# An attention and mixture-of-experts layer: who may hold which pair of PSUM banks

## The chip, the core and the metric

The kernel runs on one core of a Trainium2 chip. Its engines are TensorE (PE: matmuls, with its weight loads shown apart as PEld), VectorE (DVE), ScalarE (ACT), GpSimd (POOL) and the DMA queues of SyncE (SP). They run at the same time and wait for each other by semaphores. The metric is the time of one execution on the device in microseconds (us), less is better.

## The reference, cut to what matters

The layer takes x of 4 x 2048 tokens with 256 features. It is normalised and modulated, goes through causal attention with 16 heads of 16 features, and then through a mixture of 8 experts of which each token takes two. The part that matters here is the attention:

```python
scores = einsum('bhid,bhjd->bhij', q, k)
rel    = einsum('bhid,pd->bhip', q, rel_key)          # 512 relative positions
bias   = take_along_axis(rel, clip(j - i + p - 1, 0, p - 1))
logits = where(j <= i, (scores + bias) * scale, -inf)
out    = softmax(logits) @ v
```

## The kernel before, in words

The program has four phases: modulation, projection, attention, experts. Only the attention phase (`phase_attention`) is touched. It treats the queries in 64 blocks of 128 tokens (16 blocks in each of 4 sequences); block i of a sequence meets the key blocks j = 0 to i. A block of keys within the 512 relative positions is "near" (`near(i, j)`, five of them at most); one further off is "far". A far one has one bias for all its keys, so it needs far fewer matmuls.

Two kinds of work write to PSUM in units of one pair of banks (2 x 512 values on each of 128 partitions):

- **Scores.** For each pair of blocks (number k) two halves, t = 0 and t = 1. PE computes a half (`near_scores` L1161 and L1167, 48 matmuls; `far_scores` L1205, 8 matmuls), ACT reads it with one exponential into `att_pt` (L1126 near, L1129 far). There are 1088 such halves. The 16 matmuls of `weigh` (L1282) then multiply the weights of both halves with the values, into another bank (`att_po`).
- **Maxima.** The softmax's maxima are worked out two blocks ahead, from the same products in another layout: PE computes a half (`near_maxima` L1179 and L1185, 24 matmuls; `far_maxima` L1195, 4 matmuls), and DVE takes the running maximum of it and of `att_acc` (L1039; the first two of a block by two instructions of L1034). There are 1088 of these too, 560 near and 528 far.

Six of the eight banks form `pairs[0..2]` (NPAIR = 3). One more bank, `att_po`, gathers the output, and the last, `att_pk`, serves the single steps: turning the maxima (L1228, read by DVE at L1047), the row of maxima, and the output's normalisation, product and routing (`bank` with the kinds turn, rows, norm, back, out, turn_h, logit, count).

The order of the work is fixed in advance. A planner (`plan`, with `place_time` and `step_time`) spreads the maxima and the single steps over the places of the main loop: score half 0, score half 1, `weigh` of the pair before. `order(...)` walks it once for each engine, and all engines keep it. Before that, one walk calls `take(unit)` for each score half and each half of the maxima. It writes down which pair of banks the unit uses (`pair_of`) and which unit held that pair before (`held_by`). On PE, `pair_free` waits for the reader of the former holder: for ACT's exponential if it was a score half, for DVE's maximum if it was one of the maxima.

Of the kernel before, what the change touches and what calls it, by code (L numbers as in the profile page):

```python
# [36 lines left out]
NB = S // P  # L37
# [612 lines left out]
def phase_attention(nc, io, keep, memory, first):  # L650
# [4 lines left out]
    NPAIR, JT, LEAD = 3, 4, 6  # L655
# [113 lines left out]
    units, pair_of, held_by = [], {}, {}  # L769

    def take(unit):

        pair_of[unit] = len(units) % NPAIR
        held_by[unit] = units[-NPAIR] if len(units) >= NPAIR else None
        units.append(unit)
    order(score=lambda n, j, k, t: take(("scores", t, k)),
          bank=lambda number, behind, kind, *_: take(("maxima", number)) if kind in ("near", "far") else None)

    with memory as a:
# [982 lines left out]
```

How the kernel before makes its waits and increments, by code:

```python
def expand_across(pool, keep, att, n):  # L167
    pool.wait_ge(att.lower, n + 1)
    for part in ACROSS:
        last = expand_groups(pool, keep, att, n, part)
    last.then_inc(att.spread, 1)
    pool.wait_ge(att.spread, n + 1)
# [50 lines left out]
            @block.sync  # L224
# [6 lines left out]
                    sp.dma_start(prj.x[:, it], xv[it]).then_inc(prj.x_first[it], 16)  # L231
                for w, name in ((prj.wq, "wq"), (prj.wk, "wk"), (prj.wv, "wv")):
                    sp.dma_start(w[:, :, :], io[name].rearrange("(e p) n -> p e n", p=P)).then_inc(prj.weights, 16)
                for w, name in ((prj.bq, "bq"), (prj.bk, "bk"), (prj.r0, "r0")):
                    sp.dma_start(w[:, :], io[name]).then_inc(prj.biases, 16)
                sp.dma_start(prj.bv[:, :], io["bv"].partition_broadcast(P)).then_inc(prj.biases, 16)
                sp.wait_ge(pool_step, 1)
                sp.dma_start(io["s_odd"].rearrange("(o p) a -> o (p a)", o=1), odd.rearrange("o e u d v a -> o (e u d v a)")).then_inc(odd_out, 16)
                sp.wait_ge(odd_out, 16)
                sp.dma_start(keep["mask_q"][:, :], io["s_odd"]).then_inc(odd_in, 16)
                sp.wait_ge(odd_in, 16)
                sp.wait_ge(rel_ready, 1)
                sp.dma_start(io["s_rel"][0], relh[:, :]).then_inc(table_out, 16)
                sp.dma_start(io["s_rel"][1], rell[:, :]).then_inc(table_out, 16)
                sp.wait_ge(table_out, 32)
                for i in range(G):
                    seen = slice(G - 1 - i, G - 1 - i + TABW)
```

## Time and profile before

| | |
|---|---|
| median of 3 runs | 3443.24 us (3442.55 to 3448.19) |
| the profiled execution | 3444.56 us, of which the span of its instructions is 3442.5 us |
| busy over the span | PE 2930.0 (85%), PEld 2395.7 (70%), DVE 2277.3 (66%), ACT 1459.2 (42%), POOL 1635.0 (47%) |
| mean granted clock of TensorE | 0.936 of full speed |
| attention phase on PE | from 260.7 us to 2901.1 us |

In the profile each row names a line of the kernel, the engine and the operation, what is written and what is read. PE's time is in two rows: the weight loads (PEld) overlap the matmuls (PE). What stands in brackets behind a row is how long the engine was idle before it and which instruction ended that idle time; "issue" means that nothing in the profile explains it. A unit's matmuls overlap those of the next unit, so the distance between the starts of two units, not the sum of their durations, is what PE spends on one.

### The profile page before, as it was taken

Reading aid. Unit: us, or ns where it says so; the run is one execution under the profiler, and the core shown is the slowest. Engines: PE = TensorE matmul, PEld = TensorE weight load, DVE = VectorE, ACT = ScalarE, POOL = GpSimd, SP = SyncE. Lnnn points to the kernel's source line nnn. Section 1 sums busy time; section 2 is a strip of 40 time slices with the busy share of each in tenths; the row PEclk is TensorE's granted clock in tenths of the full one; section 3 lists DMA queues with packets and bytes.
Section 4 is the critical chain, followed back from the end, with each engine's and each line's share of the span. In section 5 each row is a group of like instructions: output and inputs, shape, how many; then the busy total and the mean of one; then the engine's idle time right before and its main releaser. Section 6 shows DMA issues by size and latency. Waiting matters only on the chain. (4 is left out here: it accounts for less than half of the span.)

```text
span 3442.5 us, 158264 instructions
## 1 busy us (share of the span) xinstructions
PE 2930.0 (85%) x70369; PEld 2395.7 (70%) x70369; DVE 2277.3 (66%) x3796; ACT 1459.2 (42%) x1765; POOL 1635.0 (47%) x1710
## 2 busy tenths in 40 slices
PE   6776899989979998998899989979999995689880
PEld 5445787777768877787787767867877774578760
DVE  6875677776357777744677777357777741666774
ACT  3551334445413344553234444613344453445551
POOL 6665644434475543345655343476444223123647
PEclk8886999999979999998999999989999997899995
DMA  4762222101321110113111110321111001634655
GB/s 117 193 169 64 60 56 54 37 22 42 88 64 45 49 46 24 36 36 107 56 39 51 33 36 24 88 71 54 39 39 36 20 13 37 217 121 153 201 167 145
DMA packets 267455, 253.62 MB, mean 74 GB/s; under 512 B 108073, under 2 KB 227726, under 8 KB 266654
## 3 DMA queue, kind: packets, MB, share of 16 engines
q1 hardware_dynamic: 245246, 201.01, 20.4%
q0 software_dynamic: 20448, 41.45, 4.1%
q8 instruction: 562, 9.21, 1.1%
q14 instruction: 111, 0.91, 0.1%
q10 hardware_dynamic: 1088, 1.05, 0.1%
HBM read 158.83 MB, written 84.46 MB: 71 GB/s over the span
## 5 line engine op out<-in xcount | busy, mean ns | idle before, releaser
L1039 DVE TENSOR_TENSOR att_acc<-att_pair,att_acc 128x1024 f16<-128x1024 f32 x960 | 1164.4, 1221 | 321.9 <-PE att_pair L1185 166.6
L1126 ACT ACTIVATE att_pt<-att_pair 128x1024 f32<-128x1024 f32 x560 | 573.1, 1023 | 1345.6 <-PE att_pair L1167 1345.6
L1282 PE MATMUL att_po<-att_pt,att_vn 128*17 128x128 f32 x17408 | 593.2, 277 | 6.3 <-ACT att_pt L1129 5.1
L1129 ACT ACTIVATE att_pt<-att_pair 128x1024 f32<-128x1024 f32 x528 | 512.3, 1024 | 187.2 <-PE att_pair L1205 183.9
L1282 PEld LDWEIGHTS att_po<-att_pt,att_vn 128*17 128x17 f32 x17408 | 435.4, 98 | 79.7 <-issue 45.4
L182 POOL TENSOR_TENSOR att_qx<-att_qe,mask_i 64x1024 f16<-64x1024 f16 x128 | 239.5, 1884 | 519.2 <-PE att_po L1282 509.7
L1161 PE MATMUL att_pair<-att_qs,att_kn 113*128 113x64 f16 x8960 | 370.8, 196 | 69.6 <-issue 37.9
L1161 PEld LDWEIGHTS att_pair<-att_qs,att_kn 113*128 113x128 f16 x8960 | 314.5, 100 | 143.6 <-issue 90.5
L1167 PE MATMUL att_pair<-att_qx,table_x 68*128 68x64 f16 x8960 | 366.3, 195 | 0.0
L1167 PE MATMUL att_pair<-att_qz,table_z 128*128 128x64 f16 x8960 | 364.4, 195 | 0.3 <-issue 0.2
L1167 PEld LDWEIGHTS att_pair<-att_qx,table_x 68*128 68x128 f16 x8960 | 312.9, 100 | 0.0
L1167 PEld LDWEIGHTS att_pair<-att_qz,table_z 128*128 128x128 f16 x8960 | 310.8, 99 | 0.6 <-issue 0.5
L1034 DVE SCALAR_TENSOR_TENSOR att_acc<-att_pair,bound 128x512 f16<-128x512 f32 x256 | 161.9, 682 | 149.6 <-PE att_pair L1185 149.6
L1179 PE MATMUL att_pair<-att_qq,att_kq 64*128 64x128 f16 x4480 | 229.7, 224 | 24.2 <-DVE att_acc L1039 10.1
L939 POOL TENSOR_TENSOR att_r<-att_ve,att_halfway 128x1 f32<-128x1 f32 x64 | 36.6, 573 | 441.3 <-DVE att_ve L1069 440.9
L182 POOL TENSOR_TENSOR att_qz<-att_qe,mask_i 128x1024 f16<-128x1024 f16 x128 | 239.1, 1884 | 0.0
L1195 PE MATMUL att_pair<-att_qq,att_kq 64*128 64x256 f16 x2112 | 205.6, 276 | 35.4 <-DVE att_acc L1039 34.9
L1185 PE MATMUL att_pair<-att_qy,table_z 64*128 64x64 f16 x4480 | 228.6, 193 | 1.0 <-issue 1.0
L1185 PE MATMUL att_pair<-att_qx,table_x 64*128 64x64 f16 x4480 | 228.5, 193 | 0.2 <-issue 0.2
L1047 DVE TENSOR_REDUCE att_mx<-att_pk 128x4 f32<-128x512 f32 x256 | 175.6, 686 | 76.8 <-PE att_pk L1228 76.2
L1442 POOL TENSOR_TENSOR moe_h_s<-moe_h_f,moe_h_s 128x512 f16<-128x512 f32 x78 | 90.6, 1161 | 254.0 <-ACT moe_h_s L1618 250.6
L1205 PE MATMUL att_pair<-att_qs,att_kn 49*128 49x128 f16 x4224 | 179.7, 217 | 31.1 <-DVE att_acc L1039 16.4
(219 smaller groups left out, 4571.5 us busy)
## 6 DMA issues: line engine op xcount, KB each, us to landing
att_qe<-s_q SPq DMA_DIRECT2D x256, 128.0 KB
moe_xs<-s_h SPq DMA_DIRECT2D x78, 256.0 KB, 3.0
s_y<-moe_y SPq DMA_DIRECT2D x78, 256.0 KB
s_v<-att_vn SPq DMA_DIRECT2D x32, 272.0 KB, 4.3
att_vn<-s_v SPq DMA_DIRECT2D x64, 136.0 KB, 3.0
s_q<-att_kq SPq DMA_DIRECT2D x64, 128.0 KB, 2.2
s_k<-att_kq SPq DMA_DIRECT2D x64, 128.0 KB, 2.4
att_qf<-s_q SPq DMA_DIRECT2D x256, 32.0 KB
```

What stands on the lines that cost most here:

```text
L182: return pool.tensor_tensor(dst[0:rows, s, :, heads, :], att.qe[0:rows, n % 2, heads].rearrange("p h (g i) -> p g h i", i=G), keep["mask_i ...
L1039: dve.tensor_tensor(held, got, held, ALU.max).then_inc(max_done, 1)
L1047: dve.reduce_max(mx[:, n % 2, :].rearrange("p (a c) -> p c a", c=QUADS)[:, r], full[:, :].rearrange("p (h k) -> p h k", k=P), AX.X).then_i ...
L1126: act.activation(pt[:, k % 2, :, t * 64:t * 64 + 64].rearrange("p h (x c) -> p x h c", x=2), full[:, :, :].rearrange("p x (h c) -> p x h c ...
L1129: act.activation(pt[:, k % 2].rearrange("p (e h) c -> p e h c", e=2)[:, :, 4 * t:4 * t + 4], full[:, :, :].rearrange("p e (h c) -> p e h c ...
L1161: pe.matmul(halves[:, x, :, h], kn[0:rows, j, h, :], qs[0:rows, s, :, h, (2 * t + x) * XQ:(2 * t + x + 1) * XQ], start=(h == 0), stop=Fals ...
L1167: last[x] = pe.matmul(groups[:, x, :, g], table[:, y:y + P], moving[:, s, (2 * t + x) * (XQ // G) + g], start=False, stop=(g == XQ // G - ...
L1179: pe.matmul(banks[:, e, c * P:(c + 1) * P], keys[rows, c, :], qq[rows, n % 2, c, :, t * XQ:(t + 1) * XQ], start=(c == 0), stop=False, skip ...
L1185: last[e] = pe.matmul(groups[:, e, g], table[:, y:y + P], moving[:, t * (XQ // G) + g], start=False, stop=(g == XQ // G - 1), skip_group_c ...
L1195: last[e] = pe.matmul(banks[:, e, 2 * c * P:(2 * c + 2) * P], keys[rows, 2 * t + c, :], qq[rows, n % 2, 2 * t + c], start=True, stop=True, ...
L1205: last[e] = pe.matmul(banks[:, e, h * P:(h + 1) * P], kn[rows, j, head, :], qs[rows, s, e, head, :], start=True, stop=True, skip_group_che ...
L1282: last = pe.matmul(po[32 * (h % 4):32 * (h % 4) + VN, h // 4, :], vn[:, j, h, :], pt[:, k % 2, h, :], start=(j == 0 and h < 4), stop=(j == ...
```

## The change

`take` no longer hands out the three pairs in rotation. Half 0 of all scores uses pair 0, half 1 uses pair 1, and all maxima use pair 2. A unit's former holder is the last unit that used the same pair (looked for among the last 128 units). The order of instructions on each engine stays as it was, as do their number, their operands' sizes and all DMAs; what differs is the bank that 2176 units write and read, and the one wait in `pair_free`.

```diff
     def take(unit):
 
-        pair_of[unit] = len(units) % NPAIR
-        held_by[unit] = units[-NPAIR] if len(units) >= NPAIR else None
+        pair_of[unit] = unit[1] if unit[0] == "scores" else NPAIR - 1
+        earlier = [u for u in units[-8 * NB:] if pair_of[u] == pair_of[unit]]
+        held_by[unit] = earlier[-1] if earlier else None
         units.append(unit)
```

## Rows read from the trace of the kernel before

**Rows 1.** Busy time, clock (before the DMA share) by stretch, of all engines.
```profile
260.00:2902.00 2642.00, 2381.64 (x66241) 1967.88 (x66241) 1747.93 (x2705) 1088.10 (x1105) 1243.24 (x1333) 0.96 0.17 47
728.00:782.00 54.00, 49.12 (x1395) 38.88 (x1389) 42.12 (x48) 26.07 (x26) 19.83 (x21) 1.00 0.10 29
950.00:1050.00 100.00, 80.03 (x1965) 69.73 (x1963) 57.43 (x115) 18.54 (x19) 66.88 (x76) 0.82 0.18 53
```

**Rows 2.** Waits of the weight loads, 250 to 2905 us: total us, times, longest.
```profile
PEld att_pair L1195 <- DVE att_acc L1039: 52.0, 81, 1.5
...
PEld att_pair L1161 <- ACT att_pt L1126: 17.4, 32, 0.9
...
PEld att_pk L1228 <- DVE att_mx L1047: 12.9, 15, 1.7
...
PEld att_pair L1179 <- ACT att_pt L1126: 0.2, 1, 0.2
```

**Rows 3.** Timeline of PE from 742 us: start, duration, what.
```profile
742.06 0.39 PE L1195 MATMUL att_pair<-att_qq,att_kq 64*128 64x256 f16 x4 [0.57 <-DVE att_acc L1039]
742.38 1.07 PE L1282 MATMUL att_po<-att_pt,att_vn 128*17 128x128 f32 x32
743.38 0.40 PE L1205 MATMUL att_pair<-att_qs,att_kn 49*128 49x128 f16 x8
743.62 0.39 PE L1179 MATMUL att_pair<-att_qq,att_kq 64*128 64x128 f16 x8
...
744.08 0.39 PE L1205 MATMUL att_pair<-att_qs,att_kn 49*128 49x128 f16 x8
744.39 1.07 PE L1282 MATMUL att_po<-att_pt,att_vn 128*17 128x128 f32 x32
745.39 0.40 PE L1179 MATMUL att_pair<-att_qq,att_kq 64*128 64x128 f16 x8
```

**Rows 4.** Timeline of DVE in the same stretch.
```profile
742.52 1.23 DVE L1039 TENSOR_TENSOR att_acc<-att_pair,att_acc 128x1024 f16<-128x1024 f32 x1
744.31 1.22 DVE L1039 TENSOR_TENSOR att_acc<-att_pair,att_acc 128x1024 f16<-128x1024 f32 x1 [0.56 <-PE att_pair L1185]
```

**Rows 5.** Timeline of PE around 759 us.
```profile
758.18 0.40 PE L1179 MATMUL att_pair<-att_qq,att_kq 64*128 64x128 f16 x8
...
759.08 0.40 PE L1179 MATMUL att_pair<-att_qq,att_kq 64*128 64x128 f16 x8
...
759.64 0.64 PE L1161 MATMUL att_pair<-att_qs,att_kn 113*128 113x64 f16 x16
...
761.15 0.39 PE L1195 MATMUL att_pair<-att_qq,att_kq 64*128 64x256 f16 x4
```

**Rows 6.** Timeline of PE from 729 us.
```profile
729.62 0.40 PE L1179 MATMUL att_pair<-att_qq,att_kq 64*128 64x128 f16 x8
...
730.53 0.40 PE L1179 MATMUL att_pair<-att_qq,att_kq 64*128 64x128 f16 x8
...
731.70 0.40 PE L1205 MATMUL att_pair<-att_qs,att_kn 49*128 49x128 f16 x8 [0.54 <-DVE att_acc L1034]
...
733.35 0.39 PE L1195 MATMUL att_pair<-att_qq,att_kq 64*128 64x256 f16 x4
733.58 0.39 PE L1205 MATMUL att_pair<-att_qs,att_kn 49*128 49x128 f16 x8
733.81 0.38 PE L1195 MATMUL att_pair<-att_qq,att_kq 64*128 64x256 f16 x4
735.34 0.40 PE L1205 MATMUL att_pair<-att_qs,att_kn 49*128 49x128 f16 x8 [1.15 <-DVE att_acc L1039]
...
736.67 0.40 PE L1179 MATMUL att_pair<-att_qq,att_kq 64*128 64x128 f16 x8
```

**Rows 7.** Timeline of DVE in the same stretch.
```profile
730.36 2.47 DVE L1034 SCALAR_TENSOR_TENSOR att_acc<-att_pair,bound 128x512 f16<-128x512 f32 x4
733.46 0.69 DVE L1047 TENSOR_REDUCE att_mx<-att_pk 128x4 f32<-128x512 f32 x1 [0.62 <-PE att_pk L1228]
734.07 2.35 DVE L1039 TENSOR_TENSOR att_acc<-att_pair,att_acc 128x1024 f16<-128x1024 f32 x2
```

**Rows 8.** Timeline of ACT, 742 to 749 us.
```profile
743.85 1.94 ACT L1129 ACTIVATE att_pt<-att_pair 128x1024 f32<-128x1024 f32 x2 [0.91 <-PE att_pair L1205]
```

## The prediction

> **What bounds the kernel now.** I read the stretches by engine first, then PE's waits, then the timeline. Attention takes 2640 of the 3442.5 us of the span, and PE is busy for 2381.6 of 2642 us there, DVE for 1747.9, ACT for 1088.1 [rows 1]. PE is the bound, but DVE is near behind: in the stretch from 728 to 782 us it is busy for 42.1 of 54 us. The waits say what little holds PE up: eleven rows, from 52.0 down to 0.2 us, are weight loads of `att_pair` that waited for ACT or DVE to release a pair of banks, 172.5 us together [rows 2]. Those are the waits that the change deals out anew. The order on PE is fixed, so a late release delays everything behind it, score halves and `weigh` included; nothing overtakes.
>
> **How long one pair is held by a maximum.** A far one: PE starts at 742.06, DVE at 742.52, and it reads for 1.23 us [rows 3, 4]. The next user of a pair starts about 0.05 us after its release (DVE's first of two ends at about 735.28, and PE's idle time at 735.34 [rows 6, 7]), so the cycle is 0.46 + 1.23 + 0.05 = 1.74 us. A near one: 743.62 to 744.31 is 0.69, with 1.22 and 0.05 that makes 1.96 us. With three pairs in rotation the next maximum rarely cares about this, as it takes another pair. With one pair for all maxima, each maximum must start a whole cycle after the one before it. What PE has to do between two maxima is the only cover.
>
> **What PE has between two maxima.** I counted in the written order what stands between each two consecutive maxima, and took the distance of starts from the rows: near maximum to far score 0.46, far score to `weigh` 0.31, `weigh` to the next 1.00, far maximum to `weigh` 0.32 [rows 3]; far maximum to far score 0.23, score to maximum 0.23 [rows 6]; near maximum, one single step, maximum 0.90; near maximum to near score 0.56, near score to maximum 1.51 [rows 5]. A single step after a far maximum I take as 0.65 (0.25 less, as for `weigh`: 0.56 against 0.32). A second far score adds 0.2. What is short is the cycle less this distance:
>
> - nothing between, 30 after a near and 16 after a far maximum: 1.5 us short each, 69 us
> - one single step on `att_pk`, 69 and 28: 1.06 and 1.09 short, 104 us
> - one `weigh`, 60 and 60 (distance 1.56 and 1.32): 0.40 and 0.42 short, 49 us
> - one far score, 20 and 8: 1.27 short, 36 us
> - two far scores, 20 and 12: 1.08 short, 35 us
> - a single step and one or two far scores, 16 and 24: 0.75 short on the mean, 30 us
> - a single step and `weigh`, 32 and 44: 0.08 short, 6 us
>
> That is 329 us from 439 of the 1087 distances. The largest class, 244 maxima with exactly one near score before them, has a distance of 0.56 + 1.51 = 2.07 against 1.96, and some 1.84 against 1.74 after a far one: it is covered, by 0.1 us only. Everything longer is covered.
>
> **What DVE's own queue adds.** DVE also reads the single steps, 0.69 us for a turn [rows 7], in the same order. Where one lies ahead of a maximum, that one is read late, and with a single pair PE can't run ahead to make up for it. I bound this by zero from below. From above, take the trace as it stands: over all 1088 maxima, the time by which the maximum before was still being read (or had not been released for 0.05 us) when the next one started adds up to 414 us, DVE's backlog included; so 85 us at most. Setting the trace's own durations again step by step, with the new releases, I get 383 us in all, that is 54 for this term, and take it. (The same done with the old releases gives 2639.6 us for the phase where the trace has 2639.3, so little is lost in it.)
>
> **What the scores get.** They never wait for DVE any more. Half t now waits for the exponential of the same half of the previous pair. Where far pairs follow with no maximum between them, ACT needs 1.94 us for two exponentials [rows 8] and PE 0.2 + 0.31 + 1.00 = 1.5 us plus whatever step stands there, so ACT can hold a half up by some 0.4 us. The layout gives that 68 times, 27 us; the bounds are 0 and 68 x 0.44 = 30.
>
> **What goes.** All 172.5 us of the old waits are replaced. The single steps wait for DVE too (18 rows for `att_pk`, the first 12.9 us [rows 2], 97 us together); since DVE is less behind when PE stands still more often, some of that goes. I put it at 28 us, from the same layout, between 0 and 97.
>
> **A stretch to check it by.** Maxima start at 729.62 and 730.53. DVE reads each of these first two by two instructions, 2.47 us for four, from 730.36 [rows 6, 7]; so the first is released at 731.60, and the second can't start before 731.65, 1.12 us later than now. The wait of 0.54 us ahead of 731.70 disappears in return. At 733.35 and 733.81 two far maxima stand 0.46 apart; the second must then come 1.74 or more after the first, and the 1.15 us ahead of 735.34 disappear. The maximum at 736.67 comes about 0.9 us later than now. So a stretch of 7 us loses 0.9: new waits are about twice as large as the ones they replace, because the unit that waits stands ahead of score work that had no need to wait.
>
> **The sum.** 329 + 54 + 27 - 172 - 28 = +210 us. The profiled execution took 3444.56 us (2 us around its span), 1.3 us above the median of 3443.24; 3443 + 210 = 3653, with TensorE's clock as it is in the phase, 0.96 on the mean [rows 1]. Rounded: 3655 us.
>
> **A rule that speaks against the change.** The rows show the price of one pair: 1.74 to 1.96 us per maximum, of which PE works on it for less than 0.7. The Trainium skill says under "Perfetto Trace Analysis", section "Optimizing Tensor Performance", that independent groups of matmuls should rotate through different PSUM banks so that reading one out overlaps the next group's matmuls. By that rule the maxima alone lose their rotation, and the scores keep one of two; it gives the direction, and no size.
>
> **Rivals.**
> *The clock falls with PE's business.* From 950 to 1050 us PE is busy for 80.0 of 100 us and the clock is 0.82, while from 728 to 782 it is busy for 49.1 of 54 (0.91) at 1.00 [rows 1]. After the change the phase has 2382/2850 = 0.84 busy. If its mean clock falls from 0.96 to 0.91, PE's work, some 2380 us, takes 130 us more, of which the waits hide a part, say 40: 3745 us. Against it: dense stretches such as 728 to 782 would still be at about 0.82 busy and the new waits are each under 2 us, spread evenly. The Trainium skill ("TensorE: Matmul & The Clock Gate", section "A second HAM failure mode: psum-queue depth-cycling") tells of a kernel that cycled through PSUM banks and lost throughput because short idle times made the clock swing; that would be this rival.
> *The waits overlap more than I think.* If the queue's term is 0 and all 97 us of the single steps' waits go, the sum is 329 + 0 - 172 - 97 = +60, 3503 us; with half of each, 3580. For it speaks that DVE idles ahead of many maxima; against it that the layout reproduces the old phase.
> *The scores win.* One mechanism with the other sign: the score halves no longer stand behind DVE, 172 us go, and the maxima, computed two blocks ahead, could be late at no cost. It would give 3443 - 172 = 3271 us. It holds only if PE could pass a waiting maximum; its price turns into a gain from the point where the new waits of the maxima are under 172 us. The 439 short distances and the rigid order speak against it: the first four classes alone hold 258 us.
> *No net change*, new waits as large as the old, within 3443 +- 7: only if DVE read the maxima in half the time that the rows show.
>
> **How the numbers follow.** My forecast (3605 to 3705) 0.68; the clock's rival (above 3705) 0.14; the overlap's (3450 to 3605) 0.13; the scores win 0.03; no net change 0.02. A measurement of this kernel tells 0.2%, about 7 us, from no change. So faster 0.03, same 0.02, slower 0.95. The range is 3590 to 3735: it leaves out the far end of either rival, about one chance in five.
>
> **What the next profile would show.** Right: the weight loads of L1179 and L1195 wait for L1039 and L1034 for 350 to 420 us together, those of L1161 and L1205 for DVE not at all, L1205 for ACT some 30; the phase ends near 3110 us; DVE's busy time is the same; the maxima stand 1.75 us apart or more after far ones. Wrong: if L1161 or L1205 still wait for DVE (the assignment isn't what I read), if the sum of these waits is right but the phase is longer (the clock), or if DVE's instructions on `att_pair` have another length (then who shares a bank matters, which no row here can show).

## The result, and the profile after

The changed kernel takes 3659.28 us (median of 4 runs, 3655.3 to 3662.9) against 3445.72 us before (3442.55 to 3449.06): a ratio of 1.0635, with a 95% interval of 1.0611 to 1.0658. It is 214 us slower. Forecast were 3655 us, 210 us slower.

The profiled execution took 3662.9 us, its span is 3660.9 us. These rows answer to [rows 1], with the same columns: the attention phase, and the 13th block of queries, which was at 728 to 782 us before.

```profile
260.00:3118.00 2858.00, 2415.74 (x66241) 1982.24 (x66241) 1769.66 (x2708) 1088.39 (x1105) 1243.19 (x1335) 0.95 0.15 43
772.00:832.00 60.00, 49.13 (x1377) 38.29 (x1372) 42.19 (x48) 26.07 (x26) 19.82 (x21) 1.00 0.09 26
```

PE starts the attention phase at 260.9 us and ends it at 3117.5 us, where it was 260.7 and 2901.1: 216 us more, so all but 2 us of what the spans differ by (3660.9 against 3442.5) lies in this phase. Of it 182 us are idle time of PE (2858 - 2415.7 against 2642 - 2381.6) and 34 us are busy time: the same 66241 matmuls took longer, at a mean clock of 0.95 against 0.96. The block shows the waits alone: 60 us for what took 54, with nearly the same work (1377 and 1395 matmuls in the two stretches), PE busy for 49.1 us of either, DVE for 42.2 and 42.1, and the clock at full speed in both.

What PE waits for is told by the waits of the weight loads. All rows for `att_pair` that name DVE or ACT, and three that name "issue" (lines are one higher than before, so L1180 is the near maxima, L1196 the far ones, L1206 the far scores):

```profile
PEld att_pair L1196 <- DVE att_acc L1040: 214.2, 248, 2.7
PEld att_pair L1180 <- DVE att_acc L1040: 152.3, 196, 2.9
...
PEld att_pair L1180 <- DVE att_acc L1035: 58.4, 46, 1.6
...
PEld att_pair L1206 <- ACT att_pt L1130: 29.5, 79, 0.7
PEld att_pair L1180 <- issue: 25.8, 97, 1.6
...
PEld att_pair L1206 <- issue: 18.5, 92, 0.2
PEld att_pair L1196 <- DVE att_acc L1035: 12.2, 32, 0.7
...
PEld att_pair L1196 <- issue: 8.9, 40, 0.5
```

Before, eleven rows with 172.5 us were spread over maxima and scores [rows 2]. Now the maxima alone wait for DVE, 437.1 us in 522 waits, and no score half waits for DVE at all; far score halves wait for ACT, 29.5 us.

The timeline shows how it comes about, at the same place of the work as [rows 6] and [rows 7]. First PE:

```profile
773.33 0.40 PE L1180 MATMUL att_pair<-att_qq,att_kq 64*128 64x128 f16 x8
...
773.80 0.39 PE L1206 MATMUL att_pair<-att_qs,att_kn 49*128 49x128 f16 x8
...
775.41 0.40 PE L1180 MATMUL att_pair<-att_qq,att_kq 64*128 64x128 f16 x8 [1.22 <-DVE att_acc L1035]
...
777.53 0.39 PE L1196 MATMUL att_pair<-att_qq,att_kq 64*128 64x256 f16 x4
777.76 0.39 PE L1206 MATMUL att_pair<-att_qs,att_kn 49*128 49x128 f16 x8
779.51 0.39 PE L1196 MATMUL att_pair<-att_qq,att_kq 64*128 64x256 f16 x4 [1.37 <-DVE att_acc L1040]
...
781.25 0.40 PE L1180 MATMUL att_pair<-att_qq,att_kq 64*128 64x128 f16 x8
```

Then DVE:

```profile
774.08 1.28 DVE L1035 SCALAR_TENSOR_TENSOR att_acc<-att_pair,bound 128x512 f16<-128x512 f32 x2
776.11 1.29 DVE L1035 SCALAR_TENSOR_TENSOR att_acc<-att_pair,bound 128x512 f16<-128x512 f32 x2 [0.76 <-PE att_pair L1186]
777.63 0.69 DVE L1048 TENSOR_REDUCE att_mx<-att_pk 128x4 f32<-128x512 f32 x1 [0.23 <-PE att_pk L1229]
778.24 1.21 DVE L1040 TENSOR_TENSOR att_acc<-att_pair,att_acc 128x1024 f16<-128x1024 f32 x1
779.97 1.22 DVE L1040 TENSOR_TENSOR att_acc<-att_pair,att_acc 128x1024 f16<-128x1024 f32 x1 [0.52 <-PE att_pair L1196]
```

The second maximum starts at 775.41, 0.05 us after DVE is done with the first (774.08 + 1.28 = 775.36). Before, it started 0.91 us after the first one; now 2.08. The fourth starts 1.98 us after the third, a far one, not 1.74: DVE was reading a single step's bank (777.63, 0.69 us) when the third was ready, so this reading began late. That is DVE's own queue, the term on which the sum was least sure. Without such a delay the cycles are the bare ones, as a little later in the same block, 1.98 us after the near maximum and 1.75 after the far one:

```profile
783.23 0.40 PE L1180 MATMUL att_pair<-att_qq,att_kq 64*128 64x128 f16 x8 [0.21 <-DVE att_acc L1040]
...
785.21 0.39 PE L1196 MATMUL att_pair<-att_qq,att_kq 64*128 64x256 f16 x4 [0.35 <-DVE att_acc L1040]
...
786.96 0.39 PE L1196 MATMUL att_pair<-att_qq,att_kq 64*128 64x256 f16 x4 [0.57 <-DVE att_acc L1040]
```

In the first stretch it was 7.05 us from the first maximum to the last (729.62 to 736.67) and is 7.92 (773.33 to 781.25), a loss of 0.87 where the prediction had "about 0.9".

### The profile page after: what moved, and what is told of

It is laid out like the page before. It is cut to its first block and busy times, and to the rows that moved or that the text cites. A ratio compares the mean times of both kernels' runs of the same rounds, so it can differ in the third digit from the quotient of the medians.

```text
span 3660.9 us, 158263 instructions
## 1 busy us (share of the span) xinstructions
PE 2967.3 (81%) x70369; PEld 2412.6 (66%) x70369; DVE 2298.0 (63%) x3796; ACT 1459.4 (40%) x1765; POOL 1634.8 (45%) x1710
## 3 DMA queue, kind: packets, MB, share of 16 engines
q10 hardware_dynamic: 1088, 1.05, 0.1%
## 5 line engine op out<-in xcount | busy, mean ns | idle before, releaser
L1040 DVE TENSOR_TENSOR att_acc<-att_pair,att_acc 128x1024 f16<-128x1024 f32 x960 | 1174.4, 1223 | 501.1 <-PE att_pair L1186 267.3
L1283 PEld LDWEIGHTS att_po<-att_pt,att_vn 128*17 128x17 f32 x17408 | 435.4, 99 | 73.1 <-issue 37.1
L1162 PE MATMUL att_pair<-att_qs,att_kn 113*128 113x64 f16 x8960 | 375.7, 197 | 28.3 <-issue 22.2
L1162 PEld LDWEIGHTS att_pair<-att_qs,att_kn 113*128 113x128 f16 x8960 | 319.6, 101 | 99.1 <-issue 87.4
L1180 PE MATMUL att_pair<-att_qq,att_kq 64*128 64x128 f16 x4480 | 231.1, 225 | 162.8 <-DVE att_acc L1040 106.2
L1196 PE MATMUL att_pair<-att_qq,att_kq 64*128 64x256 f16 x2112 | 211.7, 280 | 162.8 <-DVE att_acc L1040 157.0
L1180 PEld LDWEIGHTS att_pair<-att_qq,att_kq 64*128 64x128 f16 x4480 | 131.3, 96 | 251.2 <-DVE att_acc L1040 152.3
L1035 DVE SCALAR_TENSOR_TENSOR att_acc<-att_pair,bound 128x512 f16<-128x512 f32 x256 | 164.5, 684 | 149.0 <-PE att_pair L1186 149.0
L1196 PEld LDWEIGHTS att_pair<-att_qq,att_kq 64*128 64x128 f16 x2112 | 60.5, 94 | 247.1 <-DVE att_acc L1040 214.2
```

The costliest lines, as they stand in the source:

```text
L1035: last = dve.scalar_tensor_tensor(out=held[:, e], in0=got[:, e], scalar=LOWEST, in1=bound[:, e].unsqueeze(1).broadcast_to([P, H, XQ]), op0 ...
L1040: dve.tensor_tensor(held, got, held, ALU.max).then_inc(max_done, 1)
L1162: pe.matmul(halves[:, x, :, h], kn[0:rows, j, h, :], qs[0:rows, s, :, h, (2 * t + x) * XQ:(2 * t + x + 1) * XQ], start=(h == 0), stop=Fals ...
L1180: pe.matmul(banks[:, e, c * P:(c + 1) * P], keys[rows, c, :], qq[rows, n % 2, c, :, t * XQ:(t + 1) * XQ], start=(c == 0), stop=False, skip ...
L1196: last[e] = pe.matmul(banks[:, e, 2 * c * P:(2 * c + 2) * P], keys[rows, 2 * t + c, :], qq[rows, n % 2, 2 * t + c], start=True, stop=True, ...
L1283: last = pe.matmul(po[32 * (h % 4):32 * (h % 4) + VN, h // 4, :], vn[:, j, h, :], pt[:, k % 2, h, :], start=(j == 0 and h < 4), stop=(j == ...
```

## The experiments

They ran in three groups, each on another chip, and the kernel before took 3501.68, 3438.27 and 3500.70 us there. So only ratios to the kernel before of the same group are compared between groups.

### The wait alone, with the old banks

```diff
                     full = pair_free(("maxima", number))
+                    if number:
+                        pe.wait_ge(max_done, number)
```

> The kernel before, with its rotation of three pairs as it is; PE only waits, ahead of each half of the maxima, for DVE to have read the half before it. My theory: the whole loss is this wait (one cycle of 1.74 to 1.96 us from maximum to maximum), and it doesn't matter which banks are used. Then about +203 us over the kernel before, 3649 us, near the changed kernel's 3659. Rival 1, the placement in the banks itself (who shares a bank with whom, or the scores' tie to the same half): the rotation is kept here, so about 3446 to 3500 us. Reading on both sides: the waits of the weight loads of the maxima for DVE are some 400 us by the theory, under 150 by the rival.

Measured: 3777.43 us against 3501.68, ratio 1.0784 (1.0754 to 1.0813). The placement in the banks isn't needed for the loss: with the rotation intact, the wait is enough for the whole loss. But it is 1.5% more than the changed kernel loses, which the theory didn't give. Only 289.8 us of the waits of the maxima are put down to DVE, not 400, since two rows of "issue" have grown (L1179 to 134.0 us, L1195 to 92.7); and the releases look different. DVE, then PE, in that trace:

```profile
726.84 1.21 DVE L1039 TENSOR_TENSOR att_acc<-att_pair,att_acc 128x1024 f16<-128x1024 f32 x1
```

```profile
728.20 0.40 PE L1179 MATMUL att_pair<-att_qq,att_kq 64*128 64x128 f16 x8 [1.02 <-DVE att_acc L1039]
```

The next user starts 0.15 us after the release (728.05), not 0.05. For most waiting maxima the distance from release to weight load is 115 ns here and 53 ns in the kernels before and after. Hence two more runs.

### A control: a second wait that holds nothing up

```diff
                     full = pair_free(("maxima", number))
+                    if number > 8:
+                        pe.wait_ge(max_done, number - 8)
```

> A control for the experiment with the added wait, which came out at a ratio of 1.078 where the changed kernel has 1.064. Kernel before, rotation as it is; ahead of each half of the maxima PE also waits for the half eight before it, which was read long ago. It holds nothing up, but it is one more wait on PE's queue, 1079 times. In the trace of that experiment a maximum that waited started 115 ns after its release, against 53 ns in the other two. Theory: the excess of 1.5% is this second wait, 0.06 us each, so here 30 to 65 us over the kernel before, a ratio of 1.009 to 1.019. Rival: a satisfied wait costs nothing (ratio 1.000 to 1.002) and the excess came from the combination of old and new holders.

Measured: 3499.93 us against 3500.70, ratio 0.9993 (0.9979 to 1.0007). My theory of the excess falls in this form: 1079 satisfied waits cost nothing that can be measured.

### The wait alone, without a second one where it can be avoided

```diff
-                    full = pair_free(("maxima", number))
+                    if held_by["maxima", number] and held_by["maxima", number][0] == "scores":
+                        pair_free(("maxima", number))
+                    full = pairs[pair_of["maxima", number]]
+                    if number:
+                        pe.wait_ge(max_done, number)
```

> The added wait again (rotation of three pairs, each half of the maxima waits for the reading of the one before it), but where the former holder of the pair was also a half of the maxima, its own wait is left out, since the new one covers it: 618 of 1088 have one wait, 467 have two. Theory: the wait rule alone makes the loss, +203 us, and the second wait adds 0.06 us to less than half of them, some 15 to 25 us: ratio 1.063 to 1.068, clearly under 1.078. Rival: it stays at 1.078, and something of rotation and order together costs more than the fixed holders.

Measured: 3728.49 us against 3500.70, ratio 1.0640 (1.0618 to 1.0661), as the theory had it. The changed kernel, run beside it:

> The changed kernel once more, unaltered, on the same chip as the two others, for the comparison: a ratio of 1.061 to 1.066 by every theory.

Measured: 3724.02 us, ratio 1.0625 (1.0603 to 1.0648). The two agree within their intervals. So the wait from maximum to maximum makes the loss, whichever banks are used, and fixing the scores to their halves adds nothing that shows.

What the first variant has beyond this is explained in part. A wait that does block costs more when another stands ahead of it. This run shows both kinds side by side: where the former holder was one of the maxima, so that one wait is left, 284 weight loads start 53 ns after the release; where it was a score half, so that there are two, 194 start 115 ns after it. Between 100 and 200 ns lie 710 maxima in the first variant and 413 here, so 0.06 x 300 = 18 us, and PE's idle time in the phase is 503 and 485 us, 18 us apart. The rest shows as TensorE's clock: in the phase it stood at half speed for 358 us in the first variant and for 299 us in this one, and PE's busy time is 2463 and 2436 us, 27 us apart. Together that is the 46 us by which the two phases differ (2966 and 2920 us). That the short delays caused the lower clock is only argued; no run changes the clock alone, and the two variants ran on different chips, though the kernel before took the same time on both.

### One pair for the scores, two for the maxima

```diff
-        pair_of[unit] = unit[1] if unit[0] == "scores" else NPAIR - 1
+        pair_of[unit] = 0 if unit[0] == "scores" else 1 + unit[1] % 2
```

> The changed kernel with the holders dealt out the other way: one pair for all score halves, two pairs for the maxima in turn. Theory: what costs is a single pair with a reader behind it, whoever reads. A score half is held for about 0.4 (far) or 1.6 (near) + 1.02 + 0.1 us, and the two halves of a pair of blocks stand next to each other on PE with 0.2 us or nothing between them, so the waits of the scores for ACT are larger than those that the maxima lose: about +368 us over the kernel before, 3814 us. Rival 2, DVE alone is what PE waits for, ACT has time in plenty (it is busy for 40% of the span): the maxima have two pairs again and it is not slower than the kernel before, 3350 to 3450 us.

Measured: 3874.99 us against 3501.68, ratio 1.1061 (1.1033 to 1.1088), 373 us more. That is the theory's number (368). The maxima hardly wait any more, the scores do, for an engine that is busy for 38% of the span:

```profile
PEld att_pair L1206 <- ACT att_pt L1130: 320.0, 279, 1.4
PEld att_pair L1162 <- ACT att_pt L1127: 190.0, 235, 2.3
...
PEld att_pair L1196 <- DVE att_acc L1040: 19.0, 38, 1.5
```

So it isn't DVE as such: a single pair makes one chain of PE, reader and PE, whoever the reader is, and how busy that reader is on the mean says nothing about it.

### Reading half as long, after and before

DVE takes the running maximum of half of the heads only, so this kernel leaves out the update of half of `att_acc`; everything else is unchanged.

```diff
-                        dve.tensor_tensor(held, got, held, ALU.max).then_inc(max_done, 1)
+                        dve.tensor_tensor(held[:, :, 0:H // 2] if kind == "near" else held[:, :, 0:HH // 2], got[:, :, 0:H // 2] if kind == "near" else got[:, :, 0:HH // 2],
+                                          held[:, :, 0:H // 2] if kind == "near" else held[:, :, 0:HH // 2], ALU.max).then_inc(max_done, 1)
```

> The changed kernel, in which DVE takes the running maximum of half of the heads of each half only (the other heads keep the value of their first block); that halves the reading of 960 of the 1088 maxima, from 1.22 to an estimated 0.65 us. Theory: the cycle from maximum to maximum falls to about 1.17 to 1.39 us and most distances are covered: about -185 us, 3474 us; the waits of the maxima for DVE fall from 437 us to under 220. Rival 3, PE's clock and short idle times are the cause, or the banks themselves: the loss against the next kernel stays about 214 us.

> The same halved reading in the kernel before, to compare with. Theory: the rotation hides most of the reading already, so it gains only about 94 us, 3352 us, and the loss by the fixed holders shrinks from 214 to about 121 us. Rival 3: the two gain the same and the loss stays about 214 us.

Measured, in one group: after 3529.42 us (ratio 1.0085, 1.0060 to 1.0111), before 3415.25 us (0.9753, 0.9732 to 0.9773), with the plain kernel before at 3501.68. The reading takes 0.69 us. The kernel after comes out some 190 us below the full one (3501.68 x 1.063, an estimate for this chip; expected 185), the kernel before gains 86 us (expected 94). The loss by the fixed holders is 114 us (expected 121), where with the full reading it is some 219 on such a chip (0.0625 x 3500.70). The waits of the maxima are down to 257.9 us:

```profile
PEld att_pair L1197 <- DVE att_acc L1040: 108.7, 190, 2.1
...
PEld att_pair L1181 <- DVE att_acc L1040: 79.0, 123, 2.8
PEld att_pair L1181 <- DVE att_acc L1035: 58.0, 46, 1.6
```

(One more row has 12.2 us.) They were expected under 220, and the difference is the rows of L1035, the first maxima of each block, which still take 1.28 us: 58.0 us here, 58.4 in the changed kernel. The reading that was shortened moved the time, and the one that was not stayed. A loss by the placement would not have halved. On the clock this pair says less: PE's busy time in the phase is 2369 us before and 2378 after, only 9 us apart where it was 34 with the full reading, so the clock's part shrinks together with the waits.

### Which of the two loses its freedom

Here a small timeline in the planner gives each unit, among the pairs that it may use, the one whose reader is done first. Its core, with estimated durations for PE, DVE and ACT read from the trace before:

```diff
-    def take(unit):
...
-        pair_of[unit] = len(units) % NPAIR
-        held_by[unit] = units[-NPAIR] if len(units) >= NPAIR else None
...
+    def take(unit, may, on_pe, filled, reader, reads):
...
+        pair = min(may, key=lambda p: ready[p])
+        start = max(free["pe"], ready[pair] + 0.05)
+        free["pe"] = start + on_pe
+        free[reader] = ready[pair] = max(free[reader], start + filled) + reads
+        pair_of[unit] = pair
+        earlier = [u for u in units[-8 * NB:] if pair_of[u] == pair]
+        held_by[unit] = earlier[-1] if earlier else None
```

Maxima on pair 2 only, scores on any:

> The maxima keep pair 2 for themselves, but the score halves may take any of the three pairs, whichever is read first. Theory: the tie of the scores to their half costs nothing, since their reader ACT is done by then; the time is that of the changed kernel, 3660 us within 10. Rival 4, part of the 214 us is the scores' fixed half (29.5 us of waits for ACT and what follows from them): 3600 to 3630 us.

Measured: 3659.76 us against 3438.27, ratio 1.0642 (1.0624 to 1.0659), the changed kernel's ratio. The maxima wait for DVE for 436 us, as there (437). Freeing the scores gives nothing back.

Scores on pairs 0 and 1, maxima on any:

> The other way round: the scores are kept to pairs 0 and 1, but a half of the maxima may take any of the three, whichever is read first. Theory: one way out for the maxima gives back most of the loss: about +81 us over the kernel before, 3527 us. Rival 4: with the scores held to two pairs the loss stays near 214 us, 3630 to 3660 us.

Measured: 3507.54 us against 3438.27, ratio 1.0198 (1.0180 to 1.0215), 69 us more (expected 81). Two thirds of the loss go as soon as a maximum may step aside. What is left is of another kind: of the 259 us of waits for a release 191 are now waits for ACT, so two fixed pairs do cost the scores something once the maxima share them.

### Each unit on the pair that is free first

Scores and maxima both on any pair:

> Neither rotation nor fixed holders: a small timeline in the planner, with durations from the trace, gives each unit the pair whose reader is done first. Theory: the waits left are those that three pairs can't avoid; about 14 us less than the kernel before, 3432 us (0.4%). Rival: the rotation is as good as any, as an estimate of release times is off by more than it can win: within 7 us of 3446, or slower.

Measured: 3419.08 us against 3438.27, ratio 0.9944 (0.9931 to 0.9957), 19 us less (expected 14). The gain is small, but clear of the interval, and it beats both kernels. The waits for a release are 160 us in thirteen rows, where there were 172.5; the largest is

```profile
PEld att_pair L1185 <- ACT att_pt L1150: 28.4, 46, 1.1
```

## Why the prediction was right, point by point

**The time.** 3655 forecast, 3659 measured. The mechanism and the place were as forecast; that the time came within 4 us is in part luck, as errors in the terms cancelled. The sum adds up waits of the weight loads, so it is laid against their account of the phase: 202 us more idle time (674 to 876) and 14 us more busy time (1967.9 to 1982.2) make the 216. The terms of the sum measure 392 + 29.5 - 172.5 - 23 = 226 us (each is looked at below), 16 more than the 210 forecast. Two things are not in the sum: the 14 us of busy time, and 24 us of idle time that went besides. Of these, 18 are the "issue" rows of far scores, `weigh` and near scores (25.5, 45.4 and 90.5 us, now 18.5, 37.1 and 87.4). 226 - 24 + 14 = 216.

**New waits of the maxima: 383 forecast, 437 in the rows.** The cycles are right within 0.02 us. Read off both traces unit by unit, the median distance from a far maximum to the next rises from 0.23 to 1.74 us where nothing stands between, from 0.66 to 1.74 over one single step and from 1.32 to 1.74 over one `weigh`; from a near one it rises from 0.89 to 1.98 over one single step and from 1.56 to 1.98 over one `weigh`, where 1.96 was forecast (DVE starts 0.70 us after PE, not 0.69). The numbers of these distances (16, 28, 60, 60 and the rest) are those of the prediction's list, and the 244 with one near score keep their 1.83 and 2.07 us. In the stretch of 775 us a waiting maximum starts 0.05 us after the release. The sum went by the least distances of starts, which hold no idle time. In the trace a part of the weight loads of the maxima had waited for nothing visible before (L1179 and L1195 "issue"); it fell from 79.6 us to 34.7 (25.8 + 8.9). These are its rows of before:

```profile
PEld att_pair L1179 <- issue: 47.6, 200, 2.0
...
PEld att_pair L1195 <- issue: 32.0, 151, 0.3
```

A unit that waits for a release doesn't pay this on top. 437 - 45 = 392, against 383. The prediction's own sign for these waits was 350 to 420 us; the 437 lie above it, since it had not counted the "issue" time that they would take in.

**DVE's queue: 54, between 0 and 85.** The maximum at 779.51 shows it at work, 0.24 us over the bare cycle. Over the phase it can be read apart: for each maximum that waited for its release, how much later than the least distance (0.46 or 0.70 us) DVE had begun to read the one before. That adds up to 55 us, so the estimate was right; the short distances then have 392 - 55 = 337, against 329.

**Scores for ACT: 27 us in 68 waits; 29.5 in 79.** As forecast, and only for far scores.

**Old waits gone: 172.** All of them, as forecast: no row of L1162 or L1206 names DVE.

**Single steps: 28 less.** The rows of `att_pk` that name DVE fell from 97 to 74 us, 23 less.

**The clock.** This term was set at nothing, and it isn't nothing: PE's busy time rose by 34 us with the same instructions, the clock fell from 0.96 to 0.95 in the phase, and it stood at half speed for 287 us of it, where it was 217. How much of the 34 us lengthened the phase, and how much passed in time in which PE would have waited, no run tells; the weight loads show 14. The rival had priced a fall to 0.91 at 130 us before what waits hide, 26 us for each hundredth; so it had a part in the loss, with too large a fall. The Trainium skill ("TensorE: Matmul & The Clock Gate", section "A second HAM failure mode: psum-queue depth-cycling") tells of frequent short idle times between groups of matmuls with which the clock swings and throughput is lost. The direction agrees with this row, at a sixth of the loss; that the short waits are the cause isn't shown.

**DVE's busy time.** It was forecast unchanged and rose by 22 us in the phase (1747.9 to 1769.7), though one reading takes 1223 ns where it took 1221. Readings that follow each other at once overlap a little (2.35 us for two at 734.07 [rows 7]), and now fewer do.

**The rival of overlap.** Its sum, 329 + 0 - 172 - 97 = 60, leaves out the 27 us of waits for ACT that the main sum has; with them it is 87, 3530 us. The measurement lies far from either.

**The sign.** The rival in which the scores win took the waits of the scores as the price to save. They did go, and so did a quarter of the single steps' waits (97 to 74 us), but nothing on PE passes a waiting maximum, and the new waits are 2.5 times as large as the old.

**The rule on rotating banks** (the Trainium skill, "Perfetto Trace Analysis", section "Optimizing Tensor Performance"): the runs agree, and add where it counts. Taking the rotation from the maxima costs 6.4%, taking it from the scores 10.6%; letting the scores rotate freely beside fixed maxima gives nothing back.

## What to carry to other kernels

Before giving a buffer to one kind of work, work out its cycle (fill, reader's start, reading, release) and lay it against the distance between two fills in the written order: each distance that is shorter becomes a stall of a queue that works in order, and the mean busy share of the reader says nothing about it. A pool that all kinds share lets the slow reader's backlog spread over all pairs (before, 65 of the 172.5 us were scores that waited for DVE), but it stops PE less: 172.5 us of such waits in all, against 466.6 with fixed pairs; dealing the pairs out by which reader will be done first does a little better than turns, at no cost on the chip. When a test adds a wait, leave out the one that it makes superfluous, or the test measures two things.

## What the runs showed of the hardware

- A weight load that waits for one release starts 53 ns after it (478 of the 1088 maxima in the changed kernel, and none sooner); with another, satisfied wait ahead of the blocking one it was 115 ns (194 times in the variant without an avoidable second wait, beside 284 with one wait and 53 ns), while 1079 satisfied extra waits behind the old one cost nothing (ratio 0.9993).
- The same kernel before took 3438 us in one group of runs, 3446 in another and 3501 in two more, on chips that differ at least between the groups of experiments. DVE's mean duration of one full maximum stayed between 1220 and 1224 ns in all full kernels, and ratios held: 1.0635 and 1.0625 for the changed kernel. Between the trace of the kernel before and that of the control, which takes the same time as the kernel before on its chip, 45 of 54 us lie in the attention phase: 32 us are idle time of PE and 12 busy time, and the rows that grew most are "issue". The cause stays open.
- DVE's reading did not change with who shares its pair of banks: 1221 ns before, 1223 after.
